# A planner's prices for the TensorE array's modes, new nudges, and a later load of ones

## What is computed

```python
for layer in (0, 1):                       # L0, L1
    h = layernorm(x) * (1 + ca) + sa       # modulation from c @ wmod
    x = x + ga * attention(h)              # 16 heads of 8; softmax over 512 keys, L1 causal
    h = layernorm(x) * (1 + cb) + sb
    p = softmax(h @ gate)                  # 8 experts, the best 2 of them weigh in
    # L0: silu(h@w1[e]) * (h@w3[e]) @ w2[e] for the two, plus one shared expert
    # L1: relu(h@W1[e])**2 @ W2[e] for the two
    x = x + gb * experts(h)
```

## Time and profile before

| | us |
|---|---|
| median of 3 runs | 1134.03 |
| lowest and highest | 1131.99, 1137.25 |
| the profiled execution, its time | 1132.48 |
| its span | 1130.3 |
| PE busy in it | 1026.9 |
| DVE busy in it | 869.8 |

### The profile page before, as it was taken

One profiled execution on the slowest core, in us unless ns is written; L12 is line 12 of the kernel. 1 busy time (PEld: TensorE's weight loads), 2 busy tenths in 40 slices (PEclk: granted clock), 3 DMA queues, 4 the chain that ended last, 5 costly groups with the idle time before them and its releaser, 6 DMA issues.

```text
span 1130.3 us, 22735 instructions
## 1 busy us (share of the span) xinstructions
PE 1026.9 (91%) x8315; PEld 533.1 (47%) x8315; DVE 869.8 (77%) x1814; ACT 730.9 (65%) x1220; POOL 429.5 (38%) x484
## 2 busy tenths in 40 slices
PE   4589999889989999899889999899999889999996
PEld 2112222224555555446555566566565434455464
DVE  3799888898887888797557877777876688687455
ACT  4048766877767776666466566565657767767763
POOL 3000212354033346325135433453344468434463
PEclk9569988999999999999898999999999999999998
DMA  4804434356664777557548577695767846412110
GB/s 136 173 24 129 112 87 114 112 189 180 214 203 149 235 205 215 155 161 201 152 139 230 155 226 232 192 249 179 229 185 220 222 126 183 104 43 61 50 40 19
DMA packets 122510, 176.06 MB, mean 156 GB/s; under 512 B 20280, under 2 KB 86200, under 8 KB 122400
## 3 DMA queue, kind: packets, MB, share of 16 engines
q1 hardware_dynamic: 116064, 161.24, 49.1%
q0 software_dynamic: 5760, 12.59, 3.9%
q10 hardware_dynamic: 576, 0.79, 0.3%
HBM read 114.77 MB, written 59.67 MB: 154 GB/s over the span
## 4 chain that ended last, share of the span: by engine, by line
PE 46%; DVE 20%; DMA 15%; issue 8%; ACT 4%; POOL 3%; SPq 3%; POOLq 0%; DVEq 0%; ACTq 0%
DVE nm L965 12%; PE ps L775 10%; PE ps L837 8%; PE ps L758 5%; PE ps L736 5%; PE ps L856 5%; DMA gr<-d_y,pos 4%; PE ps L873 2%; PE ps L880 2%; DMA DR<-d_r 2%; ACT ES L1320 2%; DMA d_h<-r,pos 2%; PE ps L785 2%; DMA d_r<-DC 1%; PE ps L718 1%
## 5 line engine op out<-in xcount | busy, mean ns | idle before, releaser
L965 DVE TENSOR_REDUCE nm<-ps 128x2 f32<-128x1024 f32 (+3 forms) x512 | 507.7, 1016 | 103.5 <-PE ps L742 57.2
L1320 ACT ACTIVATE ES<-ps 128x1024 f32<-128x1024 f32 (+3 forms) x512 | 430.0, 862 | 160.3 <-PE ps L758 90.1
L775 PE MATMUL ps<-ES,VS 128*9 128x512 f32 (+3 forms) x2048 | 231.1, 528 | 0.8 <-DVE nmp L976 0.4
L736 PE MATMUL ps<-KS,QS 48*128 48x512 bf16 (+3 forms) x1024 | 183.8, 366 | 38.5 <-DVE nm L965 23.6
L758 PE MATMUL ps<-QS,KS 51*128 51x512 bf16 (+3 forms) x1024 | 178.0, 352 | 20.0 <-DVE nm L965 11.6
L837 PE MATMUL ps<-hsT,wst 128*128 128x128 f32 x1104 | 158.6, 288 | 3.7 <-DVE hdx L1158 3.4
L837 PEld LDWEIGHTS ps<-hsT,wst 128*128 128x128 f32 x1104 | 136.9, 194 | 38.6 <-issue 30.1
L758 PEld LDWEIGHTS ps<-QS,KS 51*128 51x128 bf16 x1024 | 49.6, 94 | 173.7 <-DVE nm L965 55.2
L736 PEld LDWEIGHTS ps<-KS,QS 48*128 48x128 bf16 x1024 | 50.0, 95 | 153.6 <-DVE nm L965 59.3
L1528 POOL DMA_INDIRECT gr<-d_y,pos x80 | 83.2, 1040 | 99.4 <-DMA gr<-d_y,pos 63.5
L856 PE MATMUL ps<-wst,hdx 128*128 128x128 f32 x552 | 84.7, 291 | 0.6 <-ACT hsT L1347 0.4
(11 more groups left out here) (196 smaller groups left out, 1405.4 us busy)
## 6 DMA issues: line engine op xcount, KB each, us to landing
wst<-we SPq DMA_DIRECT2D x92, 576.0 KB, 5.1
d_u<-US SPq DMA_DIRECT2D x64, 256.0 KB, 2.7
KS<-d_k SPq DMA_DIRECT2D x64, 192.0 KB, 4.8
QS<-d_q SPq DMA_DIRECT2D x64, 192.0 KB, 5.5
hs<-d_h SPq DMA_DIRECT2D x25, 256.0 KB, 4.0
d_y<-ys SPq DMA_DIRECT2D x25, 256.0 KB, 4.7
d_q<-sp SPq DMA_DIRECT2D x16, 384.0 KB
d_k<-sp SPq DMA_DIRECT2D x16, 384.0 KB, 3.4
```

The source lines that it names most:

```text
L736: mm = eng.matmul(psum[:, bank[u][a], 0:n], QS[m][r:r + KA, pr, 128 * t:128 * t + 128], KS[m][r:r + KA, pr, 0:n], start=True, stop=i < NB)
L775: mm = eng.matmul(psum[32 * a:32 * a + 9, b, q0:S], VS[i % 3][:, j, 4 * g + a, :], ES[(2 * (NT * (NG * i + g) + j) + a // 2) % NES][:, a % ...
L965: eng.tensor_reduce(nm[f][:, :].rearrange("p (a c) -> p a c", a=2)[:, :, 4 * pr + t], ps2("score", i, f, pr, t)[:, :, 0:n], AX.X, ALU.max, ...
L1320: eng.activation(ES[(2 * n + pp) % NES][:, :, 0:S - q0], ps2("bscore", i, f, g, j, pp)[:, :, 0:S - q0], ACT.Exp, scale=SC1 if i >= NB else ...
```

## The change

No step is added or taken away, and no matmul, vector operation or transfer changes its shape. The plan's numbers change, and one step gets one more predecessor:

- A change into mode "full" is charged 0.2 us in the plan, any other 0.1 us (before, 0.1 us for all). `SWITCH` counts twice for a change into "full".
- The weights of PE's steps (`p_proj`, `p_v`, `pv`, `t_mm`, `max_turn`, `f_gate`, `s_up`, `rr_mm`, `d_up`, `d_dn`), of `rr_a`, `rr_pos`, `rr_tex` and of POOL's scatters and gathers, and `LAG` of four engines.
- All of `NUDGE`: other numbers in the same places (two of its 13 lines below).
- `c_ks`, the load of ones, comes after `stack` of pass 0 instead of directly after `c_one`.

```diff
 NUDGE = {
-    "r": [-0.74, -0.04, 0.02, 0.01, -0.35, -1.37, 0.25, 0.36, 0.45, 1.63, 0.0, 0.0, 0.0, 0.0, 0.0, 0.0],
+    "r": [-1.51, -0.1, 0.46, 0.08, -0.6, -0.59, 1.12, 3.47, 1.13, 2.18, 0.0, 0.0, 0.0, 0.0, 0.0, 0.0],
...
-    "t": [-0.5, -0.89, -0.57, -1.24, -0.7, -1.24, -0.53, -0.05, 0.07, 0.0, 0.01, 0.46, -1.06, 0.77, -0.38, 1.37],
+    "t": [-0.41, -2.57, -0.87, -0.33, -0.86, -3.92, -1.61, 0.04, 0.1, 0.04, -0.19, 0.77, -2.14, 1.78, 1.42, 0.69],
...
-    LAG = {"PE": 0.48, "DVE": 0.31, "ACT": 0.33, "POOL": 0.25, "SP": 1.8}
+    LAG = {"PE": 0.43, "DVE": 0.26, "ACT": 0.28, "POOL": 0.2, "SP": 1.8}
...
-                    sw = 0.1 if e == "PE" and m != mode and w else 0.0
+                    sw = (0.2 if m == "full" else 0.1) if e == "PE" and m != mode and w else 0.0
...
-                t, sw, urg, k = min((f for f in fit if f[0] <= t0 + SLACK), key=lambda f: f[2] + SWITCH * (f[1] > 0))
+                t, sw, urg, k = min((f for f in fit if f[0] <= t0 + SLACK), key=lambda f: f[2] + SWITCH * (2 if f[1] > 0.15 else f[1] > 0))
...
-        add("SP", ("c_ks", m), 0.8, 0.1 + 0.1 * m, [("c_one",)], lag=2.5)
+        add("SP", ("c_ks", m), 0.8, 0.1 + 0.1 * m, [("c_one",), ("stack", 0, 1)], lag=2.5)
...
-            add("PE", ("p_proj", i, n), 0.95, u, [x] + ready, opens=1)
+            add("PE", ("p_proj", i, n), 0.86, u, [x] + ready, opens=1)
...
-            add("PE", ("max_turn", i, f), 0.2, u, [done[-1]], opens=1)
+            add("PE", ("max_turn", i, f), 0.11, u, [done[-1]], opens=1)
...
-                add("PE", ("pv", i, g, j), 0.12 + 0.86 * n / 512, u + 0.06, exps[-2:] + [("p_vs", i)] + ([("pv", i, g, j - 1)] if j else []), mode="cols", opens=int(j == 0))
+                add("PE", ("pv", i, g, j), 0.008 + 0.857 * n / 512, u + 0.06, exps[-2:] + [("p_vs", i)] + ([("pv", i, g, j - 1)] if j else []), mode="cols", opens=int(j == 0))
...
-        add("PE", ("t_mm", i), 0.95, u, [("t_o", i), ("ld", "bo"), after_t(i - 1)], opens=1)
+        add("PE", ("t_mm", i), 0.9, u, [("t_o", i), ("ld", "bo"), after_t(i - 1)], opens=1)
...
-                add("PE", ("s_up", i, n, 0), 0.9, u, [("f_ht", i), ("ld", "fs"), ("s_dn", i - 1), ("s_gate", i - 1, n)], opens=1)
+                add("PE", ("s_up", i, n, 0), 0.98, u, [("f_ht", i), ("ld", "fs"), ("s_dn", i - 1), ("s_gate", i - 1, n)], opens=1)
...
-            add("PE", ("rr_mm", q), 0.4, u, [("rr_oh", q), ("c_more", 1)], opens=1)
-            add("DVE", ("rr_a", q), 1.25, u, [("rr_mm", q)], closes=[("rr_mm", q)])
+            add("PE", ("rr_mm", q), 0.07, u, [("rr_oh", q), ("c_more", 1)], opens=1)
+            add("DVE", ("rr_a", q), 0.8 + 0.08 * size, u, [("rr_mm", q)], closes=[("rr_mm", q)])
...
-                    add("POOL", ("r_sc", q, t, c), 1.28, u, [sent[-2], ("rr_pos", q), ("r_hx", first + t // NT), ("c_h", (max(MT) - 1) // 12)]
+                    add("POOL", ("r_sc", q, t, c), 1.35, u, [sent[-2], ("rr_pos", q), ("r_hx", first + t // NT), ("c_h", (max(MT) - 1) // 12)]
```

26 lines of the change are left out of this document (13 added, 13 removed), and 14 rows, old and new, of the table NUDGE.

## The result

The changed kernel took 1144.07 us in the median of 12 executions, the kernel before 1132.38 on the same chip: a ratio of 1.011 with an interval of 1.008 to 1.014. A second comparison on another chip gave 1.008 (1.0045 to 1.011). I had predicted 1125.5, so the sign is wrong. The profiled execution took 1140.56 us with a span of 1138.8, 8.5 us over that of before. The ratios leave out the few executions that took over 1.5% more than the fastest of their kernel.

The account below looks back on a forecast made before the run. PE's own work was taken to bound the kernel from 225 to 1073 us. Mode changes -10.0, start -0.5, pass 6 with the third group +2 gave -8.5 us: a median of 1125.5 us, range 1109 to 1139.

Parts of the forecast that it names:

- What bounds the kernel: From 225 to 1073 us, PE's own work sets the time; it idles for only 42.3 of 848 us.
- The price and number of the mode changes: Runs cost 0.19 (full), 0.10 (half), 0.09 us (cols); fewer runs save PE 10.3 us, taken as -10.0 in time.
- The start: Pass 0: stores issued ahead of the ones and an earlier `p_mid` bring the stacks forward; -0.5 us, bounds -1.5 and 0.
- Pass 6: PE's 4.21 us wait before `t_mm` can go, but fewer steps stand ahead of it; -4.2 to +4.8 us.
- The third group: Fewer steps between `rr_mm` and `x_turn`, so PE may wait for scatters; 0 to +10.2 us, +2 together with pass 6.
- The work was not the bound: Rival: each us saved on PE is given back at its next wait; 1133.5 us, no change; chance 0.15.
- The scatters decide, slower: Rival: PE waits for scatters at `x_turn` of the third and first groups; +15.5 us, 1149.5; chance 0.13.
- the sign of being wrong: PE's busy time falls and its idle time rises as much, above all before `x_turn` of the first and third group.
- The end: Last `pv` of pass 15 about 8.5 us earlier, with the same 57 us behind it.

Follow-up runs that it names:

- lighter loads: From the fifth expert tile of the first layer on, only a third of an expert's weights loaded: 0.9886 of before in before's order, 0.9858 in the changed kernel.
- the run that joined the steps: Before's plan with 29 PE steps moved by one to five places behind a neighbour of the same mode: 0.9994 of before.
- the four steps set later: Changed kernel with pass 7's norm (ACT), a combining step of pass 0 (DVE) and two `x_turn` (PE) moved later: 1131.78 us, 1.0020 of before.
- four orders drawn anew: The changed kernel (1.011 of before) and its variants planned with old mode prices (1.0369), old nudges (1.0283), and old lags with new nudges (1.0252).
- the order with the old lags: Changed kernel's mode prices and loads of ones, planned with the old lags and a nudge table made anew for them: 1.0252 of before.

## Why the prediction was wrong, point by point

**What bounds the kernel: the step that failed.** I read PE busy for 805.7 of 848 us and concluded that its own work sets the time, so that the 10 us of saved mode changes arrive at the end. A busy share says that an engine has little idle time, not that its work can shrink with the end following. 7 us of mode changes taken out of before's order brought 0.7; 20 us less of work brought 1.2, 20 us more cost 9. With lighter loads the same cut brought 13.3. That fits other chains, with landings in them, that lay just under PE's work. The Trainium skill, Perfetto Trace Analysis, Identifying the Most-Contended Engine, reads the same way as I did: the engine that is occupied most is to be improved first, with a warning that for TensorE matmul busy time is not a good measure of how near it is to its roofline. The runs here show a third thing, that occupancy does not say what a saving is worth; they do not test the warning.

**The price and number of the mode changes: right as work.** PE's busy time fell by 11.0 us against 10.3. Of that, 3.1 stand ahead of 225 us, where the clock was granted at 0.91 instead of 0.85, so the match is better than it should be. The prices of the earlier trace rows hold: a run of four expert steps in after takes 0.77 + 0.67 + 0.67 + 0.77 = 2.88 us by them, and 588.24 to 591.11 = 2.87 by the rows:

```profile
588.24 2.94 PE L837 MATMUL ps<-hsT,wst 128*128 128x128 f32 x24
591.11 0.39 PE L758 MATMUL ps<-QS,KS 51*128 51x512 bf16 x2
```

With one price for every change, 0.09 us, the same run would take 2.77; the trace speaks for two. The Trainium skill, TensorEngine Tiling (Array Packing), Key Properties, says that a change of tiling mode drains TensorE, and gives no price. The failure is in what the saving is worth at the end: -10.0 in my sum, and within 3.6 us of nothing in the run that joined the steps.

**The start: mis-sized, but inside the bounds.** -0.5 taken, bounds -1.5 and 0. The first `score` came 1.9 us earlier in this pair of traces and 1.2 in the mean of eight traces against seven. I had asked only when the stacks are issued, not how long they take to land.

**Pass 6: right, with some luck in the size.** The wait of 4.21 us went to 0.44. In the other traces with before's queue on SP it was anything from nothing to 4.4 us (4.39, 4.29, 4.11, 1.90, 0.30, and none in three), so the full 4.21 was there to be saved only in some executions.

```profile
545.17 1.16 PE L785 MATMUL ps<-w0s,OT 128*128 128x128 f32 x8 [0.44 <-DVE OT L987]
```

**The third group: inside the bounds.** `rr_mm` at 538.51 and `x_turn` at 584.96 stand 46.5 us apart, where I had 43.6 for the steps. The wait was 1.53 us of at most 10.2, since the chain took less than in the earlier trace rows:

```profile
538.51 0.19 PE L820 MATMUL ps<-ohb,before 128*128 128x64 bf16 x1
...
543.56 1.14 POOL L1504 DMA_INDIRECT d_h<-hx,pos  x1 [12.70 <-DVE pos L1135]
```

Pass 6 and this group together came to -3.8 + 1.5 = -2.3 us, for +2 taken: the right places, and the sign of the sum wrong.

**The rivals.** "The work was not the bound" was the right account of the main term; it had 0.15. "The scatters decide, slower" had the right sign and the wrong place: `x_turn` of the third group waited 1.5 us and that of the first not at all. The longest wait was behind a small step, `p_rstd`, that stands among the scatters on POOL. I looked at who waits for the scatters' data and not at who stands in the same queue. What I had written as the sign of being wrong, busy time down and idle time up by as much, is what the profile shows, only elsewhere than at those two `x_turn`.

**The end.** The last `pv` of pass 15 started at 1080.54, 7.2 us later than in the earlier trace rows, and 58.3 us stand behind it for 57.0.

**The sum by what was measured:** from 60 us to the last `pv` of pass 15, PE's busy time fell by 12.8 us and its idle time rose by 19.8, which is the 7 us by which that `pv` came later; 1.3 more lie behind it. Two steps failed. The saving on PE, -10.0 in my sum, was there as work and worth about nothing in time. And new waits of PE outside pass 6 and the third group, which no term held, because I took PE to get its inputs as before: waits in the new order cost more than the whole saving. 17.3 us of the idle time are waits of 1 us and less. Of these, the ones that `rowmax` ended did not grow (18.9 us before, 18.1 after); those that `expo` ended went from 7.4 to 12.0, and 6.3 stand where the profile shows nothing that PE waited for, with the rest spread thin. Why the new order has more of them is open: the four steps set later and the lighter loads each took the loss away, but in both the short waits stayed at 43.8 us or more, where traces of before's order have 35.0 to 41.9.

## What to carry to other kernels

Ahead of pricing a saving on the busiest engine, read the shares of the chain that ended last. Where transfers or other engines hold half of it, a saving in that engine's work has a value between nothing and its length, and only a cut of both tells. In a kernel of in-order queues, look at every step that waits for a landing (scatter, gather, combining step) and list what stands behind it on the same engine; a small step there, needed by a third engine, can cost more than the data that is waited for. Sum the waits of both kernels, long and short apart, ahead of blaming the longest new ones: the old order has its own, which go. A reordering puts all such neighbourhoods at stake. Here four orders drawn anew lost between 9 and 42 us, however good the planner's own end looked.

## What the runs showed of the hardware

**Clock and waits.** The two levels stand in the rows at 380 to 390 us of after. `pv` takes 1.05 us (380.41) ahead of the 5.24 us wait and 1.89 behind it (388.13), 2.4 and 1.2 GHz. The granted clock was 0.78 and 0.88 in the two stretches of 10 us, then 1.00:

```profile
380.00:390.00 10.00, 4.58 (x28) 0.59 (x26) 4.24 (x5) 3.84 (x7) 6.59 (x9) 0.78 0.37 115
390.00:400.00 10.00, 10.00 (x70) 6.39 (x67) 7.09 (x12) 7.04 (x11) 3.65 (x4) 0.88 0.63 202
400.00:410.00 10.00, 10.00 (x78) 5.01 (x77) 7.87 (x15) 8.15 (x15) 6.55 (x8) 1.00 0.76 241
```

So a wait costs more than its length. Here (0.22 + 0.12) x 10 = 3.4 us at full clock are missing on top, part of them while PE stands. Time and mean granted clock go together among the executions of one kernel too: the changed kernel, taken again, ran from 1134.4 us at 0.963 to 1149.6 at 0.956 and 1149.1 at 0.950. And the order with the old lags had 1046.9 us of busy time on PE for nearly the same work, at a mean clock of 0.931:

```profile
PE 1046.9 (89%) x8315; PEld 542.2 (46%) x8315; DVE 877.9 (75%) x1814; ACT 730.2 (62%) x1220; POOL 429.3 (37%) x484
```

**Traffic and landings.** With 34 of 176 MB less, a gather landed in 3.3 to 3.4 us in the median of three traces, where twelve with all of the traffic have 3.4 to 3.9, and the whole kernel was 12.9 us faster with every compute engine's work the same. The Trainium skill, DMA: Bandwidth & Descriptors, Latency and other measured facts, says that the latency of the memory is the largest part of a DMA's fixed cost and that this cost gets smaller under a lighter load; the medians lean the same way, by 0.3 us in the mean. A part of a us on a landing can count, since the 16 scatters of a group are a chain of waits for landings, 33.6 to 45.4 us long.
